# The last expert block of a four-layer decoder: routing weights spread by 32-row tile products in pairs, units in fours, TensorE's loop written out

## What is computed

```python
logits = x @ router_w.T + expert_bias[None, :]
probs = jax.nn.sigmoid(logits)
top_w, top_idx = jax.lax.top_k(probs, TOP_K)                  # TOP_K = 8
top_w = top_w / (jnp.sum(top_w, axis=-1, keepdims=True) + 1e-09) * 2.5
combine = jnp.zeros((T, 160)).at[jnp.arange(T)[:, None], top_idx].set(top_w)
h1 = jax.nn.silu(jnp.einsum('th,eih->eti', x, w_gate))        # inner width 64
h1w = h1 * combine.T[:, :, None]
routed = jnp.einsum('eti,ehi->th', h1w, w_down)
shared = jax.nn.silu(x @ w_gate_shared.T) @ w_down_shared.T
```

## Time and profile before

| | |
|---|---|
| median of three runs | 1122.97 us |
| the profiled execution's own time | 1125.25 us |
| its span | 1123.3 us |
| TensorE products (PE) busy | 960.0 us, 85% |
| VectorE (DVE) busy | 783.4 us, 70% |
| ScalarE (ACT) busy | 627.3 us, 56% |
| the chain that ended last, share of PE | 72% |
| the last expert block's loop | about 857 to 1111 us of the span |

### The profile page before, as it was taken

How to read it: one execution, slowest core, us unless ns; L and a number is a source line. 1 busy time by engine, 2 the same in 40 slices (tenths; PEclk the granted TensorE clock), 3 DMA queues, 4 the chain that set the end, 5 groups by cost and what they waited for, 6 DMA issues and landing times.

```text
span 1123.3 us, 15610 instructions
## 1 busy us (share of the span) xinstructions
PE 960.0 (85%) x5200; PEld 611.2 (54%) x5200; DVE 783.4 (70%) x1171; ACT 627.3 (56%) x1053; POOL 197.8 (18%) x150
## 2 busy tenths in 40 slices
PE   7989859997897536598898399999778999999998
PEld 3666526664354212265355277777245777777774
DVE  3466447777595767577487667776548888888886
ACT  6356425555455515255565255555457777777776
POOL 0011031321000000000100522421310333333330
PEclk9899979999999758679899699999888999999999
DMA  7000000110000000000000101101100111111100
GB/s 302 1 1 0 1 28 15 42 49 1 1 2 1 0 1 0 0 1 2 0 2 2 49 1 49 48 1 38 37 0 1 37 38 40 53 37 37 37 19 19
DMA packets 9706, 27.95 MB, mean 25 GB/s; under 512 B 1344, under 2 KB 2624, under 8 KB 9536
## 3 DMA queue, kind: packets, MB, share of 16 engines
q1 hardware_dynamic: 9664, 27.37, 7.0%
HBM read 26.84 MB, written 0.52 MB: 24 GB/s over the span
## 4 chain that ended last, share of the span: by engine, by line
PE 72%; DVE 17%; ACT 8%; issue 2%; DMA 0%; POOL 0%; DVEq 0%; ACTq 0%; SPq 0%
PE ps L624 13%; PE ps L626 12%; PE ps L625 12%; PE ps L478 4%; PE ps L470 4%; PE ps L1230 3%; PE ps L184 2%; PE ps L495 2%; PE ps L489 2%; ACT rstd L215 2%; ACT rstd L218 2%; PE ps L193 1%; ACT arena L1300 1%; PE ps L1043 1%; PE ps L994 1%
## 5 line engine op out<-in xcount | busy, mean ns | idle before, releaser
L624 PE MATMUL ps<-parts 128*128 128x512 f32 (+2 forms) x608 | 282.6, 465 | 9.5 <-DVE parts L840 6.4
L626 PE MATMUL ps<-parts 128*128 128x512 f32 (+2 forms) x608 | 242.1, 398 | 0.0
L625 PE MATMUL ps<-parts 128*128 128x512 f32 (+2 forms) x608 | 239.9, 395 | 0.0
L654 ACT ACTIVATE parts<-ps 128x512 fp32r<-128x512 f32 (+1 forms) x256 | 153.1, 598 | 152.9 <-PE ps L626 77.3
L658 DVE TENSOR_TENSOR parts<-ps,parts 128x512 fp32r<-128x512 f32 (+1 forms) x256 | 176.2, 688 | 3.0
L624 PEld LDWEIGHTS ps<-parts 128*128 128x128 f32 (+2 forms) x608 | 116.1, 191 | 47.5 <-DVE parts L658 16.2
L1802 DVE TENSOR_TENSOR ps<-arena,ps 128x512 f32<-128x512 f32 x160 | 111.3, 696 | 33.3 <-DVE parts L658 32.8
L642 POOL TENSOR_TENSOR parts<-ring,zeros 128x1024 fp32r<-128x1024 f32 (+4 forms) x52 | 72.4, 1405 | 345.7 <-PE ps L626 312.9
L626 PEld LDWEIGHTS ps<-parts 128*128 128x128 f32 (+2 forms) x608 | 113.7, 187 | 28.9
L625 PEld LDWEIGHTS ps<-parts 128*128 128x128 f32 (+2 forms) x608 | 114.7, 189 | 23.4
L845 DVE TENSOR_TENSOR ps<-arena,ps 112x512 f32<-112x512 f32 (+1 forms) x96 | 66.8, 696 | 56.4 <-PE ps L626 56.4
(11 more groups left out here) (325 smaller groups left out, 1291.5 us busy)
## 6 DMA issues: line engine op xcount, KB each, us to landing
ring<-m_in SPq DMA_DIRECT2D x20, 512.0 KB, 3.5
ring<-m_up_in SPq DMA_DIRECT2D x8, 448.0 KB, 3.6
pack<-pack_in SPq DMA_DIRECT2D x1, 2058.5 KB, 9.7
ring<-m_up_in SPq DMA_DIRECT2D x8, 256.0 KB, 2.6
ring<-m_down_in SPq DMA_DIRECT2D x8, 224.0 KB, 3.6
ring<-m_down_in SPq DMA_DIRECT2D x8, 128.0 KB, 2.5
pack<-pack_in SPq DMA_DIRECT2D x1, 968.0 KB, 14.0
pack<-pack_in SPq DMA_DIRECT2D x1, 836.0 KB, 11.2
```

The source lines that it names most:

```text
L624: nc.tensor.matmul(dst, w_high, x_high, start=start, stop=False, skip_group_check=True)
L625: nc.tensor.matmul(dst, w_high, x_low, start=False, stop=False, skip_group_check=True)
L626: return nc.tensor.matmul(dst, w_low, x_high, start=False, stop=stop, skip_group_check=True)
L654: nc.scalar.activation(m_hh[0:rows, p], ps[0:rows, src, :], ACT.Copy).then_inc(R(t, "_hh"), 1)
```

## The change

The routing weights are laid out in groups of 32 rows (10 experts in three parts, 30 rows), so a spread needs 32 rows of the array. Two spreads of different experts, on neighbouring row groups, are issued one behind the other. The order of the units changes with it: unit n is now the pair of experts `2 * (n // 4) + n % 2` on half `n % 4 // 2`. The spreads write into four banks (4 to 7) in turn, and hidden overwrites its own bank in place, so its wait for `_hl` goes. TensorE's loop is gone: all 160 steps are written out. In step n TensorE issues gate(n+3), down(n), and in every second step the spreads of units n+3 and n+4. ScalarE and VectorE loop over four units a turn. `sel160` shrinks from 20 to 5 blocks of 128 columns, and the layout of `t_parts` and the order of the expert weights in HBM follow.

```diff
+EG = SETE // 4
+PAIRS = EG // 2
+M3_UNITS = NE
...
-        sel160 = sb("sel160", [P, 20 * P], BF16)
+        sel160 = sb("sel160", [P, PAIRS * P], BF16)
...
-            def body(i, final):
-                for u in range(2 * CHUNKS):
-                    n = 2 * CHUNKS * i + u
-                    j, p = (u + 3) // 2, (u + 1) % 2
-                    if j < CHUNKS:
-                        gate(i, j, p, n + 3)
-                        spread(i, j, p)
...
-                    down(u // 2, u % 2, n, final and u >= 2 * CHUNKS - 2)
+            def gate(n):
+                q, p = unit(n)
+                if q % 4 == 0 and p == 0:
+                    wait("_split", q // 4 + 1)
+                if n >= 2:
+                    wait("_hid", n - 1)
+                mm3(bank(2 + n % 2), *weights(q, 0), half(m_xh, p), half(m_xl, p), True, True).then_inc(R("m3", "_gate"), 1)
+            def spread(n):
+                for r in range(2):
+                    q, p = unit(n + r)
+                    s, h, i = q // (4 * PAIRS), q // (2 * PAIRS) % 2, q // 2 % PAIRS
+                    at = slice(32 * (2 * h + r), 32 * (2 * h + r) + 32)
+                    ins = mm(bank(4 + (n + r) % 4), sel160[at, i * P:(i + 1) * P], half(t_combT[at, s, :], p), start=True, stop=True,
+                             tile_position=(32 * (2 * h + r), 0))
+                ins.then_inc(R("m3", "_spread"), 1)
...
-            for p in range(2):
-                wait("_wT", p + 1)
-                spread(0, 0, p)
             wait("_wT", SETS)
-            gate(0, 1, 0, 2)
-            spread(0, 1, 0)
-            with pe.Fori(0, GROUPS - 1) as i:
-                body(i, False)
-            body(GROUPS - 1, True)
+            spread(0)
+            spread(2)
+            gate(2)
+            for n in range(M3_UNITS):
+                if n + 3 < M3_UNITS:
+                    gate(n + 3)
+                down(n)
+                if n % 2 == 1 and n + 3 < M3_UNITS:
+                    spread(n + 3)
...
-            def m3_hidden(n, p):
-                if not isinstance(n, int) or n >= 2:
-                    waits(dve, "m3")("_hl", n - 1)
-                waits(dve, "m3")("_silu", n + 1)
-                waits(dve, "m3")("_spread", n + 1)
-                V.tensor_tensor(bank(6 + p), t_sg[:, p], bank(4 + p), ALU.mult).then_inc(R("m3", "_hid"), 1)
+            def m3_hidden(i, u):
+                waits(dve, "m3")("_silu", 4 * i + u + 1)
+                waits(dve, "m3")("_spread", 2 * i + u // 2 + 1)
+                V.tensor_tensor(bank(4 + u), t_sg[:, u % 2], bank(4 + u), ALU.mult).then_inc(R("m3", "_hid"), 1)
```

More of the change, by code:

```diff
@@ L1216, in _ @@
             wait = waits(pe, "m3")
[L1218 to L1224, removed]
-                if not isinstance(n, int) or n >= 2:
-                    wait("_hid", n - 1)
-                mm3(bank(2 + p), *weights(j, 0), half(m_xh, p), half(m_xl, p), True, True).then_inc(R("m3", "_gate"), 1)
@@ L1229, in spread, with unit @@
[L1229 to L1233, removed]
-                wait("_hl", n + 1)
-                mm3(bank(p), *weights(j, P), m_hh[:, p], m_hl[:, p], False, final).then_inc(S("y_ready") if final else R("m3", "_down"), 1)
-            def body(i, final):
-                for u in range(2 * CHUNKS):
-                    n = 2 * CHUNKS * i + u
-                    j, p = (u + 3) // 2, (u + 1) % 2
-                    if j < CHUNKS:
-                        gate(i, j, p, n + 3)
-                        spread(i, j, p)
-                    elif not final:
-                        gate(i + 1, j - CHUNKS, p, n + 3)
-                        spread(i + 1, j - CHUNKS, p)
-                    down(u // 2, u % 2, n, final and u >= 2 * CHUNKS - 2)
+            def unit(n):
+                return 2 * (n // 4) + n % 2, n % 4 // 2
@@ L1249, in _, with down @@
+            def down(n):
+                q, p = unit(n)
+                wait("_hl", n + 1)
+                final = q == NE // 2 - 1
+                mm3(bank(p), *weights(q, P), m_hh[:, n % 2], m_hl[:, n % 2], False, final).then_inc(S("y_ready") if final else R("m3", "_down"), 1)
             wait("_xl", 2)
             pe.wait_ge(S("m3_route"), 3)
-            for p in range(2):
-                gate(0, 0, p, p)
+            for n in range(2):
+                gate(n)
             for s in range(SETS):
@@ L1445, in _, with m3_silu, m3_high, m3_body @@
                     act.wait_ge(S("m3_route"), 4 + SETS * k + s + 1)
[L1446 to L1448 removed]
+                    A_(t_part(s, k), by_group(t_w[:, :, s * SETE:(s + 1) * SETE]), ACT.Copy).then_inc(R("m3", "_parts"), 1)
+            def m3_silu(n, u):
                 waits(act, "m3")("_gate", n + 1)
[L1450 to L1467 removed]
+                A_(t_sg[:, u % 2], bank(2 + u % 2), ACT.Silu).then_inc(R("m3", "_silu"), 1)
+            def m3_high(n, u):
+                if isinstance(n, int) and n == M3_UNITS - 1:
+                    act.wait_ge(S("y_ready"), 2 * (LAYERS - 1) + 1)
+                elif not isinstance(n, int) or n >= 2:
+                    waits(act, "m3")("_down", n - 1)
+                hidden_high(act, "m3", n, u % 2, P, 4 + u)
+            def m3_body(i, final):
+                for u in range(4):
+                    m3_high(4 * i + u, u)
+                    if not (final and u >= 2):
+                        m3_silu(4 * i + u + 2, u)
+            for n in range(2):
+                m3_silu(n, n)
+            m3_body(0, False)
+            with act.Fori(1, M3_UNITS // 4 - 1) as i:
+                m3_body(i, False)
+            m3_body(M3_UNITS // 4 - 1, True)
             log_tables()
@@ L1975 @@
         sel8[3 * e:3 * e + 3, e, :] = 1
-    sel160 = np.zeros((P, 20, 2, 64), np.float32)
-    for q in range(20):
+    sel160 = np.zeros((4, 32, PAIRS, 2, 64), np.float32)
+    for q in range(PAIRS):
         for el in range(2):
-            sel160[(2 * q + el) * 3:(2 * q + el) * 3 + 3, q, el, :] = 1
-    pairs = np.array([[20 * (j // 2) + 10 * (j % 2) + g for j in range(CHUNKS)] for g in range(GROUPS)])
+            sel160[:, (2 * q + el) * 3:(2 * q + el) * 3 + 3, q, el, :] = 1
+    pairs = np.array([[[[(s * 4 + 2 * h + r) * PAIRS + q for r in range(2)] for q in range(PAIRS)] for h in range(2)]
+                      for s in range(SETS)]).reshape(GROUPS, CHUNKS)
     gate = i["L3_ffn_w_gate"].reshape(NE // 2, P, P).transpose(0, 2, 1)
```

36 lines of the change are left out of this document (18 added, 18 removed).

## The result

The changed kernel took 1130.51 us in the median of 20 runs (1124.89 to 1134.67), the kernel before 1125.97 us in 20 runs of the same measurement (1118.09 to 1127.99). The ratio is 1.0047, with an interval of 1.0032 to 1.0062: +5.3 us, between +3.6 and +7.0. That is slower, by just under the 0.5% that the prediction called no change. (The two medians differ by 4.5.) A second measurement of the same kernel gave 1.0029 (1.0004 to 1.0055).

The account below looks back on a forecast made before the run. TensorE was taken to bound the kernel. Pairs +4.0 us, loop start +0.4 and loop end -0.2 made +4.2 on a median of 1122.97: 1127.2 us, range 1118.5 to 1136, likeliest 1124 to 1130.5.

Parts of the forecast that it names:

- What bounds the kernel: In the last block's loop TensorE sets the beat, 1.613 us a unit; VectorE has 0.75 us of slack, so shortening it gains nothing.
- The pair's stretch: TensorE from the gate product before two 32-row spreads to the second product behind: 0.96 to 0.99 us, 0.03 to 0.07 more per pair.
- The price without a row: Bf16 load of a 32-row spread, not shown in the earlier trace: taken as 0.01 us, at most 0.10.
- The 32-row load is not fast: Rival, chance 0.18: the spread's load costs 0.10 us instead of 0.01, adding 7 us, 1134.5 us in all.
- The pair costs one slot: Rival, chance 0.13: tile-size changes are free in the loop, two units take 3.00 us, 18 us less, 1105 us.
- Only the load behind the pair stays hidden: Rival, chance 0.12: the load of the product after the spreads isn't exposed, saving 0.10 us per pair, 1119 us.
- The clock falls or comes late: Rival, chance 0.05: TensorE's standstills lower its clock; 3 us more at 1.2 GHz at the start costs 1.5 to 3 us.
- The start: At the loop's beginning a switch, a load and a product lie between the last copy and hidden: +0.4 us.
- ACT and DVE have the same element counts in the routing part: Step on the routing part ahead of the loop: equal element counts on both engines, no cost added.
- The sum: Whole kernel: +4.0 us for pairs, +0.4 at the loop's start, -0.2 at its end, giving 1127.2 us.
- likeliest case: The prediction's own forecast of 1127.2 us for the whole kernel, chance 0.52, with a band of 1124 to 1130.5 us.

## Why the prediction was right, and what it missed

**What bounds the kernel: right.** TensorE's distances set the beat. VectorE lost its wait for itself, 30 us of 230, and nothing came of it, in the change and with the in-place banks alone.

**The pair's stretch: right.** The forecast was 0.96 to 0.99 us from L635 to L634. By the trace it is 0.321 + 0.003 + 0.314 + 0.335 = 0.973, and less two ordinary distances of 0.231 that is 0.51 for a pair, inside 0.49 to 0.52. The terms: entering 0.09 over an ordinary distance, leaving 0.10, the bare load of L633 0.10. The kernel with single tiles, where the same terms come twice as often, came out at +4.3%, and the one with 64 rows at the same gaps. One reading behind the terms was loose: rows 6 are not two products but the two passes of one (L184 has two products and four such records), so 0.43 is one f32 pass. The 0.21 that was taken from it for a bf16 stream holds all the same: full spreads behind each other start 0.216 apart.

**The price without a row: at its lower end.** The load of a 32-row spread was put at 0.01 and bounded by 0.10. At the start of the loop, where four spreads run from rest, the second pair starts 0.226 us behind the first. Of four full-height spreads in the same place the second also starts 0.226 behind the first, whose load was bare, and the third and fourth, whose loads were hidden, 0.216 behind the one before. So a bare bf16 load costs 0.01, with 32 rows as with 128. *The 32-row load is not fast* is out. The Trainium skill, "TensorE: Matmul & The Clock Gate", section LDWEIGHTS, has a load last its columns over 1.2 GHz, an estimate of 0.107 us for these 128 columns. The load's record lasts 0.09 here, near to that, but it costs the distance 0.01; a bare f32 load of 128 columns has a record of 0.19 and shows 0.10 in the distance.

**The first two rivals: out.** *The pair costs one slot* would have needed free changes of size, and both were paid. *Only the load behind the pair stays hidden* falls with L633, which lasts 0.50 and whose load starts with it. The Trainium skill, "TensorEngine Tiling (Array Packing)", section Key Properties, says that a change of the tiling mode drains TensorE. The gaps on both sides of the pair, 0.09 and 0.10 us, agree with it, though no run tells a drain from another wait.

**The clock: half right.** *The clock falls or comes late* happened at the start of the loop in the first profile of the change, 1.3 us, and not in the second. Pauses of 0.2 us in the loop didn't bring it about: the window over the whole loop is at 0.99 and 1.00. Every profile here has a stretch at 1.2 GHz where the routing part ends; whether it reaches into the loop differs between executions of one kernel.

**The start: about right.** "+0.4" was 0.46 by the third gate, which begins 1.34 us behind the last copy and not 0.88, and 0.55 by hidden: a pair from rest needs the copy's signal, the load, the product and its end, 0.59 behind the copy, where it was 0.03 before.

**"ACT and DVE have the same element counts in the routing part": this step failed**, though only by 0.5 us. The counts are equal and the durations are not: 783 ns against 742 in ACT's splitting, with the fourth dimension in the pattern, and 9.72 us against 9.22 from there to the last copy. DVE's splitting lasts 489 and 490 ns, so it is no part of it.

**The sum.** The +4.0 for the pairs was 0.060 x 78 = +4.7, at the upper end of the step's +2.4 to +5.5. With the start the loop came to +5.0, where 4.0 + 0.4 = 4.4 was forecast; behind the last down product it is -0.1 (8.94 us against 9.07), where -0.2 was forecast; ahead of the loop +0.5, where nothing was. That is +5.4 for a forecast of +4.2, and the runs say +5.3 in one measurement and +3.3 in the other, which can't tell the two apart.

**The absolute time and the chances.** The forecast's 1127.2 lies 3.3 below the measured median, of which 3.0 is that the kernel before had a median of 1125.97 in that measurement and 1122.97 in the three runs known then. The measured 1130.51 lies in the range of 1118.5 to 1136, but just outside the likeliest case's own 1124 to 1130.5. Read as a time it is "slower by over 0.5%", which had 0.37; read as a ratio it is "within", which had 0.47. So the close ratio is earned by the terms, and the place of the time in the range owes as much to where the kernel before stood that day. Two small slips in the rivals: the third one's +7 on 1127.2 is 1134.2 and not 1134.5, and 0.097 more in each of 79 pairs is some 7.7, so the sum by the page's load time is nearer +12 than +11.

**What the prediction didn't see** is a part that its comparison hid. It priced the pair against two spreads apart, which is right for the total. But the change also brings two spreads together, and that, with the later start paid, is worth -2.8 us in the loop. The tiles cost 0.107 us per pair against the same order, 7.8 us, and the order gave 2.8 of it back. Nothing in the trace of before shows two bf16 products together among split products, so the gain could have been bounded only by the scatter of the distances in the earlier trace rows, 0.22 to 0.24.

Still open: whether the gap of 0.09 to 0.10 on each side is one and the same wait or two different ones, and why the distance of split products depends on what runs around them (fewer changes between bf16 and split products is one guess that no run tested).

## What to carry to other kernels

Row tiles side by side save time only where several of them follow one another: here a change between full-height products and smaller tiles costs about 0.09 us going in, 0.10 coming out, and 0.10 for a bare load behind it, together 0.29, which is more than the one 512-column product saved. By an estimate from these numbers two pairs in a row would save about 0.45 for the same 0.29; no run had that inside the loop. Take a change apart by running its pieces alone: here the tile was a loss and the new order, which came along with it, a gain, and the order alone, with full-height products and the old layout of the weights, was faster than the kernel before, by 0.25% in one measurement and 0.5% in the other. Measure a stretch inside one trace (copy to last product) when the runs scatter by more than the effect looked for.

## What the hardware showed that was not expected

- Identical split products start 0.228 us apart in the mean where the bf16 spreads stand in twos, 0.230 where they stand alone and 0.231 beside 32-row tiles. Twos against alone is 0.026 us in two units, 2 us in all, and with the 0.02 at the spreads themselves 3.7.
- A bare bf16 load costs 0.01 us though its record lasts 0.09 to 0.10, with 32 and with 128 rows alike; a bare f32 load costs 0.10, with a record of 0.19.
- Two pairs of 32-row spreads from rest take 0.60 us as x4 in the changed kernel. The same four spreads with full rows take 1.04, as this timeline of the kernel with full rows and the old layout shows:

```profile
857.01 1.04 PE L1243 MATMUL ps<-arena,sel 128*128 128x512 bf16 x4 [0.79 <-DVE arena L1802]
857.75 1.29 DVE L1807 TENSOR_TENSOR ps<-arena,ps 128x512 f32<-128x512 f32 x2 [0.80 <-PE ps L1243]
```

Hidden then begins 0.80 us behind the copy and not 0.59. Where tiles follow tiles they do save the time of whole products: the second pair starts 0.226 us behind the first, as the second full spread does behind its first.

- Splitting 320 elements a partition takes ACT 733 to 750 ns with three dimensions in the pattern and 782 to 792 with four.
- The granted clock where the routing part ends differed between executions of one kernel: at 0.50 from 843.3 to 853.5 us and full from there on in one, at 0.50 again from 860 to 863 us, inside the loop, in the other, which moved the loop by 1.3 us.
